# Channel attention: inverting the softmax sums in 128x32, the gate in the values' copy, normalised rows by GpSimd

## The reference

```python
q, k, v = (W @ layernorm(x) + b, ...)             # k and v from the context
dot  = einsum('bhdt,bhds->bhts', q, k) / sqrt(8)
mask = target_mask[:, :, :, None] * source_mask[:, :, None, :]
dot  = mask * dot - (1 - mask) * 1e6
amap = softmax(dot, axis=-1) * mask
out  = einsum('bhts,bhds->bhdt', amap, v)         # 16 heads x 8 rows = 128 x 256
x    = x + tanh(g_xattn[0]) * out
```

## Time and profile before

| | |
|---|---|
| median of 3 runs | 1793.42 us (1790.8 to 1793.77) |
| profiled execution, first to last instruction | 1830.3 us, 34413 instructions |
| granted TensorE clock, mean | 0.972 of full speed |
| busy: PE, PEld | 1720.2 us (94%), 1436.8 us (78%) |
| busy: DVE, ACT, POOL | 1141.9 us (62%), 965.4 us (53%), 567.8 us (31%) |
| this attention stage | from the start to about 335 us |

### The profile page before, as it was taken

The page is one execution under the profiler, slowest core; times in us unless marked ns, Lnnn a source line. Parts: engine busy times, 40 slices in busy tenths (PEclk is TensorE's granted clock), DMA queues, the critical chain, the costliest instruction groups (busy, mean ns, idle before and its releaser), DMA issues. The chain is left out here.

```text
span 1830.3 us, 34413 instructions
## 1 busy us (share of the span) xinstructions
PE 1720.2 (94%) x11824; PEld 1436.8 (78%) x11832; DVE 1141.9 (62%) x2556; ACT 965.4 (53%) x2526; POOL 567.8 (31%) x624
## 2 busy tenths in 40 slices
PE   8999997698999999999999999999999988788988
PEld 6666664458788888888888888888888876677876
DVE  5899988897456556566566555555555668533334
ACT  2688875596455544445455455444454446244433
POOL 3233325534512111112121111111111226556664
PEclk8999997899999999999999999999999998898999
DMA  5011122102100100101001110001000034423337
GB/s 201 14 37 37 37 83 94 58 6 97 50 12 13 47 1 21 40 1 36 24 12 36 35 40 24 13 13 35 1 13 1 1 75 136 123 84 98 110 92 280
DMA packets 48825, 97.45 MB, mean 53 GB/s; under 512 B 7370, under 2 KB 29050, under 8 KB 47668
## 3 DMA queue, kind: packets, MB, share of 16 engines
q1 hardware_dynamic: 40071, 72.57, 12.9%
q0 software_dynamic: 7584, 21.37, 3.9%
q10 hardware_dynamic: 1000, 1.26, 0.2%
HBM read 73.85 MB, written 20.97 MB: 52 GB/s over the span
## 5 line engine op out<-in xcount | busy, mean ns | idle before, releaser
L2288 POOL TENSOR_TENSOR hold_wq<-hold_wq,ca_rsum 128x512 f32<-128x512 f32 x128 | 133.2, 1041 | 794.6 <-DVE ca_rsum L2530 794.6
L2141 ACT ACTIVATE hold_wq<-hold_wq,ca_nb,ca_evens 128x128 f32<-128x128 f32 x256 | 124.2, 486 | 226.9 <-DVE ca_nb L2525 226.9
L2141 ACT ACTIVATE hold_wq<-hold_wq,ca_nb,c_rqs 128x128 f32<-128x128 f32 x256 | 124.2, 486 | 222.2 <-DVE ca_nb L2525 222.2
L1054 DVE TENSOR_REDUCE a_mx<-a_s 128x2 f32<-128x512 f32 x256 | 167.4, 683 | 35.0 <-PE a_s L904 33.5
L797 ACT ACTIVATE a_prob<-a_s 128x512 f32<-128x512 f32 x256 | 148.2, 604 | 62.7 <-PE a_s L924 62.3
L2305 PE MATMUL ca_qk<-early_x,cw_wqkv_h 128*128 128x512 f32 x384 | 162.0, 422 | 1.2 <-PEq L1507 1.2
L2307 PE MATMUL ca_qk<-early_x,cw_wqkv_l 128*128 128x512 f32 x384 | 151.7, 395 | 0.0
L2306 PE MATMUL ca_qk<-early_x,cw_wqkv_h 128*128 128x512 f32 x384 | 151.3, 394 | 0.0
L2426 PE MATMUL ca_acc<-ca_wo_h,ca_oT_h 128*128 128x256 f32 x512 | 145.7, 285 | 0.2 <-DVE ca_oT_l L2539 0.2
L2427 PE MATMUL ca_acc<-ca_wo_l,ca_oT_h 128*128 128x256 f32 x512 | 144.8, 283 | 0.0
L2428 PE MATMUL ca_acc<-ca_wo_h,ca_oT_l 128*128 128x256 f32 x512 | 144.7, 283 | 0.0
(11 more groups left out here) (537 smaller groups left out, 4890.6 us busy)
## 6 DMA issues: line engine op xcount, KB each, us to landing
early_big<-slot_results SPq DMA_DIRECT2D x16, 512.0 KB
mw_raw<-in_d_expert_w SPq DMA_DIRECT2D x12, 352.0 KB, 5.6
a_wraw<-a_heads SPq DMA_DIRECT2D x32, 128.0 KB
a_heads<-a_osb SPq DMA_DIRECT2D x124, 32.0 KB
mw_down<-in_d_expert_d SPq DMA_DIRECT2D x1, 2816.0 KB
token_rows<-early_rows SPq DMA_DIRECT2D x1, 2176.0 KB, 16.1
hold_wk<-in_c_wkT SPq DMA_DIRECT2D x1, 2064.0 KB
hold_wq<-in_c_wqT SPq DMA_DIRECT2D x1, 2064.0 KB
```

What stands on the lines that cost most here:

```text
L1054: dve.tensor_reduce(mx[:, b % 2, :, h], s1_bank(b, u)[:, :, :], AX.X, ALU.max)\
L2141: ins = act.activation(prob[:, p, b, :], prob[:, p, b, :], ACT.Exp, bias=nb[:, p, b:b + 1], scale=row_scale[layer][:, r:r + 1], accum_out= ...
L2288: pool.tensor_tensor(prob[:, k % 2, :, :], prob[:, k % 2, :, :], rsum[:, k % 2, :].unsqueeze(2).broadcast_to([P, GB, TOKENS]), ALU.mult)\
```

## The change

1. The sums no longer go through `a_heads`. All eight rows of sums of a head are alike, so one of them is taken: four DMAs (`send_sums`) move the sums of 16 heads and 256 positions from four partitions of `osb` into a tile of 128x32, inside SBUF. VectorE inverts that in one instruction. SyncE stores the inverses in DRAM (`store_inverse`, ahead of `maxima`) and loads them back spread over the 128 channel rows, each head's 8 times (`spread_inverse`, behind `maxima`). The outputs go through `a_heads` as before. Batch 15 keeps the old way.
2. VectorE's inversion stands at slot 16b+48 in place of 16b+55 and 16b+57.
3. tanh of the gate is the scale of ScalarE's copy of v (`read_v`), and no longer multiplied into the mask. The masks of batches 0 to 9 are used where they lie; from batch 10 on ScalarE still copies the mask (`keep_mask`), because its place is needed by the next layer.
4. From batch 2 on GpSimd normalises the rows (x - mean) * rstd in one instruction, and ScalarE doesn't. VectorE's preparation for it (`mean_bias` at slot 26) goes.

```diff
+        SUMS = A_HEADS * DIM // P
+        sums = s.sb("sums", [P, 2, SUMS])
+        isums = s.sb("isums", [P, 2, SUMS])
...
+        inverses = nc.dram_tensor("a_inverses", (2, A_HEADS, DIM), F32, kind="Internal").ap()
...
-        CLOSING = 33
+        OWN_MASK = 10
+
+        def mask_of(b):
+            return tm[:, b, :] if b < OWN_MASK else tgm[:, b % 2, :]
+        CLOSING, INVERTED = 33, 9
...
+        def send_sums(eng, p):
+            for r in range(A_SLOTS):
+                a = A_ROWS * r + A_HD
+                eng.dma_start(sums[A_ROWS * r:A_ROWS * r + A_ROWS, p, :],
+                              osb[a:a + 1, p, :, :].rearrange("o j (c n) -> o (j c) n", n=SUMS)).then_inc(gathered[p], 16)
...
                     sp.wait_ge(out_copied, 2 * b + 2)
                     if b >= 2:
-                        sp.wait_ge(moved[p], 32 * i)
+                        sp.wait_ge(moved[p], 16 * i)
+                    if b < BATCHES - 1:
+                        if b >= 2:
+                            sp.wait_ge(inverted, b - 1)
+                        send_sums(sp, p)
                     send(sp, p, 0)
-                    if b < BATCHES - 1:
-                        send(sp, p, 1)
-                    sp.wait_ge(sent[p], 128 * (i + 1))
+                    sp.wait_ge(sent[p], 64 * (i + 1) if b < BATCHES - 1 else 64 * i + 128)
                     after(sp, x_done, 3 * (b - 1))
-                    sp.dma_start(den[:, p, :], heads[p, 1]).then_inc(moved[p], 16)
+                    if b == BATCHES - 1:
+                        sp.dma_start(den[:, p, :], heads[p, 1]).then_inc(moved[p], 16)
                     sp.dma_start(num[:, p, :], heads[p, 0]).then_inc(moved[p], 16)
+
+                def store_inverse(b):
+                    p, i = b % 2, b // 2
+                    sp.wait_ge(inverted, b + 1)
+                    if b >= 2:
+                        sp.wait_ge(spread, 16 * (b - 1))
+                    sp.dma_start(inverses[p].rearrange("h n -> (h n)").rearrange("(p n) -> p n", p=P), isums[:, p, :])\
+                        .then_inc(stored[p], 16)
+
+                def spread_inverse(b):
+                    p, i = b % 2, b // 2
+                    sp.wait_ge(stored[p], 16 * (i + 1))
+                    after(sp, x_done, 3 * (b - 1) + 1)
+                    sp.dma_start(rden[:, :], inverses[p].unsqueeze(1).broadcast_to([A_HEADS, A_HD, DIM]))\
+                        .then_inc(spread, 16)
...
                     gather(b)
+                    if b < BATCHES - 1:
+                        store_inverse(b)
                     if b + 2 < BATCHES:
                         maxima(b + 2)
+                    if b < BATCHES - 1:
+                        spread_inverse(b)
...
                 def close(b):
-                    pool.wait_ge(rden_ready, 2 * b + 2)
-                    pool.wait_ge(tgm_ready, b + 1)
+                    pool.wait_ge(spread, 16 * (b + 1))
+                    pool.wait_ge(moved[b % 2], 16 * (b // 2 + 1))
...
-                    pool.tensor_tensor(add[:, :], add[:, :], tgm[:, b % 2, :], ALU.mult).then_inc(x_done, 1)
+                    pool.tensor_tensor(add[:, :], add[:, :], mask_of(b), ALU.mult).then_inc(x_done, 1)
...
+                def normal_x(b):
+                    pool.wait_ge(rstd_ready, 2 if b >= FIRST else 1)
+                    after(pool, xm_ready, b - 1)
+                    pool.tensor_scalar(xn[:, b % 2, :], x_sb[:, b, :], mv[:, b, 0:1], rstd[:, b:b + 1],
+                                       ALU.subtract, ALU.mult).then_inc(xn_ready, 1)
...
                     if b is not None and t % U == 2:
+                        normal_x(b)
                         centre_x(b)
...
-                                   ACT.Copy).then_inc(v_ready, 1)
+                                   ACT.Copy, scale=tg[:, 0:1]).then_inc(v_ready, 1)
...
-                    act.activation(tgm[:, b % 2, :], tm[:, b, :], ACT.Copy, scale=tg[:, 0:1]).then_inc(tgm_ready, 1)
+                def keep_mask(b):
+                    act.wait_ge(ld_m[1], 16)
+                    if b >= OWN_MASK + 2:
+                        act.wait_ge(x_done, 3 * (b - 2) + 2)
+                    act.activation(tgm[:, b % 2, :], tm[:, b, :], ACT.Copy).then_inc(tgm_ready, 1)
...
-                    if prepared(t) is not None and u == 0:
-                        normal_x(prepared(t))
                     if copied(t) is not None:
-                        if copied(t)[1] == 0:
-                            gated_mask(copied(t)[0])
+                        if copied(t)[1] == 0 and copied(t)[0] >= OWN_MASK:
+                            keep_mask(copied(t)[0])
                         copy_out(*copied(t))
...
-                def invert(b, k):
+                def invert(b):
+                    p, i = b % 2, b // 2
+                    dve.wait_ge(gathered[p], 64 * (i + 1))
+                    if i > 0:
+                        dve.wait_ge(stored[p], 16 * i)
+                    dve.reciprocal(isums[:, p, :], sums[:, p, :]).then_inc(inverted, 1)
...
-                    if closed(t + 2) is not None:
-                        invert(closed(t + 2), 0)
-                    if closed(t) is not None:
-                        invert(closed(t), 1)
-                        if closed(t) == BATCHES - 1:
-                            close_last()
+                    if closed(t + INVERTED) is not None and closed(t + INVERTED) < BATCHES - 1:
+                        invert(closed(t + INVERTED))
+                    if closed(t + 2) == BATCHES - 1:
+                        invert_last(0)
+                    if closed(t) == BATCHES - 1:
+                        invert_last(1)
+                        close_last()
```

More of the change, by code:

```diff
@@ L463, in attend_channels @@
         rden_ready, x_done, vT_blank = s.sem("rden_ready"), s.sem("x_done"), s.sem("vT_blank")
+        gathered, stored = ([s.sem(f"{n}{p}") for p in range(2)] for n in ("gathered", "stored"))
+        inverted, spread = s.sem("inverted"), s.sem("spread")
         heads = nc.dram_tensor("a_heads", (2, 2, P, DIM), F32, kind="Internal").ap()
+        inverses = nc.dram_tensor("a_inverses", (2, A_HEADS, DIM), F32, kind="Internal").ap()
         U = A_HEADS
@@ L522, in attend_channels @@
         MEASURED, CONDENSED = 4, 17
-        REST_POW, REST_BIAS = 21, 26
+        REST_POW = 21
         GRAM_SLOTS = {0: (0, 24), 2: (239, 16)}
@@ L646, in _ @@
                         sp.wait_ge(v_psum, BATCHES)
-                        sp.wait_ge(tgm_ready, 14)
+                        sp.wait_ge(tgm_ready, 14 - OWN_MASK)
                         tern.load(sp)
@@ L684, in close @@
                 def close(b):
-                    pool.wait_ge(rden_ready, 2 * b + 2)
-                    pool.wait_ge(tgm_ready, b + 1)
+                    pool.wait_ge(spread, 16 * (b + 1))
+                    pool.wait_ge(moved[b % 2], 16 * (b // 2 + 1))
+                    if b >= OWN_MASK:
+                        pool.wait_ge(tgm_ready, b - OWN_MASK + 1)
+                    else:
+                        pool.wait_ge(ld_m[b >= FIRST], 16)
                     after(pool, x_done, 3 * b)
@@ L719, in _ @@
                     if t == FILLED:
-                        pool.wait_ge(tgm_ready, 14)
+                        pool.wait_ge(tgm_ready, 14 - OWN_MASK)
                         pool.wait_ge(s2_psum, U * 14)
@@ L784, in read_maxima @@
                         .then_inc(mT_ready, 1)
-                def gated_mask(b):
-                    act.wait_ge(ld_m[b >= FIRST], 16)
-                    after(act, x_done, 3 * (b - 2) + 2)
-                    act.activation(tgm[:, b % 2, :], tm[:, b, :], ACT.Copy, scale=tg[:, 0:1]).then_inc(tgm_ready, 1)
+                def keep_mask(b):
[3 more added lines that the diff above has]
+                    act.activation(tgm[:, b % 2, :], tm[:, b, :], ACT.Copy).then_inc(tgm_ready, 1)
                 def exponential(w):
@@ L803, in copy_out @@
                     if half == 0 and b >= 2:
-                        act.wait_ge(sent[b % 2], 128 * (b // 2))
+                        act.wait_ge(sent[b % 2], 64 * (b // 2))
+                        act.wait_ge(gathered[b % 2], 64 * (b // 2))
                     act.activation(osb[:, b % 2, 2 * half:2 * half + 2, :], out_bank(b, half)[:, :, :], ACT.Copy)\
@@ L832, in _ @@
                 act.wait_ge(out_copied, 2 * BATCHES)
-                act.wait_ge(moved[p], 32 * i)
                 send(act, p, 1)
@@ L1055, in take_max, with invert_last @@
                         .then_inc(max_ready, 1)
-                def invert(b, k):
+                def invert(b):
[4 more added lines that the diff above has]
+                    dve.reciprocal(isums[:, p, :], sums[:, p, :]).then_inc(inverted, 1)
+                def invert_last(k):
+                    b = BATCHES - 1
                     c = slice(P * k, P * k + P)
-                    dve.wait_ge(moved[b % 2], 32 * (b // 2 + 1))
+                    dve.wait_ge(moved[b % 2], 16 * (b // 2 + 2))
```

(6 more changed lines are left out.)

2 lines of the change are left out of this document (removed).

## The result

The changed kernel is a little slower: 1799.17 us, median of 13 runs, against 1795.99 for the kernel before, also 13 runs on the same chip. The ratio is 1.0030, with a 95% interval of 1.0016 to 1.0043, so about 5.4 us (3 to 8). The forecast was no difference, 1792.7.

What follows compares the result with a forecast made beforehand. The prediction took a circle through the maxima's DMA transfers to bound the loop at 15.59 us a batch. Loop 0 and tail -0.7 us, from a median of 1793.4, gave 1792.7 us, own range 1791 to 1794, with rivals 1788 to 1798.

Steps and rivals of the forecast that it cites:

- The circle through the maxima: Loop: ScalarE's copy of the maxima, SyncE's four transfers, TensorE's matmuls and ScalarE's next chain set the 15.59 us period.
- the reading of 167.83 against 167.60: TensorE, loop: the matmul needing the maxima starts at 167.83, its slot pair at 167.60, read as a wait for them.
- SyncE's queue: Loop: longer sums' issues and the store still leave SyncE free 0.9 us early, 0.2 at worst, before the maxima: 0.
- ScalarE, "0": Loop: removing normalisation and gated mask gains 0, since TensorE then waits for the maxima, whose time is unchanged.
- Its other end: ScalarE, loop: the removed gated mask gains the whole 0.40 us for 10 batches, 4.0 us.
- VectorE, "0": Loop: two reciprocals of 0.94 us replaced by one taken as 0.3 gain 0; the far end was 10.4 us.
- The 0.41 that the view puts to VectorE's maxima: TensorE, loop: a gap at 159.98, also at 163.58 under "issue"; said to follow the 16 matmuls ahead, whoever is named.
- GpSimd, "0": Loop: one more operation a batch, at most 1.04 us, costs 0 because GpSimd waits 5.9 us of each period.
- The tail, -0.65: Tail: SyncE's queue becomes the end, last reciprocal at 330.9 against 331.55 us; VectorE's own bound was 330.1.
- Rival B: SyncE, loop: maxima leave late if a sums' send takes over 0.80 us to issue; 1798 us at 0.9; chance 0.14.
- Rival C: Tail: the store's 128-byte pieces land in 4.4 us instead of 2.2, tail loses 1.5, 1795 us; chance 0.06.
- Rival A: Loop: the freed engines do bound it; 1788.7 us with ScalarE's end and the tail, 1778 with VectorE's too; chance 0.2.

Runs made afterwards that it cites:

- rest_only: The kernel before with the gate in the values' copy, plain mask and rows normalised by GpSimd, sums as before: 1792.3 us, ratio 0.9986 to the kernel before.
- one_before: The kernel before with one transfer for the maxima of a batch in place of four: 1795.0 us, ratio 0.9999 to the kernel before.
- sums_only: The change with only its sums' path; gate in ScalarE's mask copy and rows normalised on ScalarE as before: 1800.2 us, ratio 1.0025 to the kernel before.
- sums_in_one: The change with the sums of a batch gathered by one transfer in place of four: 1794.3 us, ratio 1.0005 to the kernel before.
- x_store: The kernel before with an unused store of 128-byte pieces to DRAM added behind the maxima; run once for its trace: period 15.59 us, 13 periods 208.09 us.
- one_mask: The kernel before with one maxima transfer, gate in the values' copy and plain mask for batches 0 to 9; trace only: period 15.40 us, 13 periods 205.72 us.
- one_sums: The kernel before with one maxima transfer per batch and, of the change, only the sums' path: 1791.9 us, ratio 0.9993 to the kernel before.
- one_rest: The kernel before with one maxima transfer, gate in the values' copy, plain mask, rows normalised by GpSimd, sums as before: 1791.7 us, ratio 0.9993 to the kernel before.
- one_all: The change with one maxima transfer, the store of the inverses behind it, and the sums gathered by one transfer: 1789.5 us, ratio 0.9979 to the kernel before.

## Why the prediction was wrong, point by point

*The circle through the maxima: right for the change, misread for the kernel before, wrong in its use.* In the change it sets the period: over issues of 2.44 (rest_only), 2.50 and 2.57 the period is 13.14 plus their length. In the kernel before TensorE did not wait for the maxima; the reading of 167.83 against 167.60 cost nothing (one_before), and ScalarE's mask held the same 15.58. That the two have one length is not explained. But the circle had, as the prediction read it, no slack (rest_only, sums_only). What follows from no slack is that 0.13 us more anywhere on it is 0.13 on every batch. The prediction checked only whether SyncE would be free in time, and held the maxima's own issues at 2.44 without saying that this was an assumption: they took 2.58.

*SyncE's queue, "0": the step that failed.* The sums' issues were put at 0.57 and took 0.62; the spare was put at 0.9 and is 0.63 (167.40 to 168.03). Both are close, and neither did the harm. The harm was done by two effects of the four added issues that no row of before shows: the first two of the maxima's issues grow (taken singly, 0.59 and 0.58 to 0.67 and 0.63 in the periods shown), and single stores take 0.77 to 1.68 us. Price in the change's quietest profile, of the stretch's 3.3 us: the long issues make twelve periods some 0.12 longer, 1.4; slow issues make two periods late by 1.0; the late landing makes one late by 0.9. The first two go with the four issues: sums_in_one has no slow issue, and issues of 2.50. For the landing this is not shown: a smaller one stands in x_store, which has no sums' issues (a period of 15.92). What late maxima do to the clock comes on top: with it the stretch is 8 and 13 us longer in the two other profiles.

*ScalarE, "0": right, by the reason given:* in rest_only TensorE waits for the maxima instead. Its other end (0.40 for ten batches, believed only if the maxima did not bind) is what one_mask shows when they don't: 0.18 a batch, 2 us in all.

*VectorE, "0": right.* one_sums alone does not settle it, since ScalarE's limit stands there too; one_rest does, with both limits gone and the reciprocals still there. The 0.41 that the view puts to VectorE's maxima stands unchanged in one_all, where VectorE has less to do: as argued, it is not a wait for VectorE.

*GpSimd, "0": right.* one_rest and one_mask differ by 0.03 us in the stretch, and by where the rows are normalised.

*The tail, -0.65: came +0.2.* VectorE does wait for its transfer, as forecast. The mis-sized terms are on SyncE: release 6.02 after the first send where 5.64 was counted, and a store of 1.57 us where 0.43 was. The release is as late in the two other profiles, 6.03 and 6.07; the store is not the whole of the rest, since the latest tail, 18.65, has a store of 0.37.

*Rival B* had the right place and the wrong point. It asked for a sums' issue over 0.80 us; at 0.62 its neighbour on the queue already cost. *Rival C* did not happen; its sign, a later last reciprocal, came by slow issues. The 128-byte store lands a median of 1.8 us after its issue begins, less than the 2.2 of the sends:
```profile
L657 SPq DMA_DIRECT2D a_inverses<-a_isums x15: 367/374/1571, 88.8 to 326.3; - x15
...
DMA to landing us min/median/max: 1.7/1.8/3.3
```
The rule of the Trainium skill, "DMA: Bandwidth & Descriptors" (Specifications), that a transfer wants 512 bytes or more for its full rate, does not show in the landing at this size of 16 KB. *Rival A* was half right, and hidden: an engine that the change freed is a limit, but only once the maxima are out of the way.

*What stays open.* Why four issues of the sums make issues of other transfers on the same queue longer, why one in three stores is slow, and why one batch's maxima land late, no view shows. Nor is the share of half clock in the 5.4 us known: three profiles are no mean.

## What to carry to other kernels

When a circle has no slack, hold nothing on it constant: ask of each edit on the same queue what it does to the neighbours' own issues, not only whether the queue is free in time. Two limits of equal length hide each other, so an edit that gains nothing alone can gain with another; take both away before calling an engine's work free. Where a batch is late, ask whether it was issued late or landed late before naming the cause. Four small transfers that one transfer can replace cost more than their own issue time.

## What was not expected of the hardware

The time that SyncE takes to issue a transfer depends on what else it issues: 0.59 or 0.67 us for the same first transfer of the maxima, and 0.37 or up to 1.68 for the same store, with 128-byte stores alone (x_store) at 0.44. Nor is the time from issue to landing fixed: the same batch's maxima came 2.08 us after their issues where others take 1.16, with a packet on the queue called "instruction" under way. A late transfer can be paid twice: 0.9 us became 5.3 by way of TensorE's clock, which went to 0.50 after TensorE had been busy 3.53 and 3.29 of 4 us; in another profile a wait of the same 1.17 us left the clock at 1.00.
